# State products on two row halves of the array, gated channel blocks in half-bank pieces, and one FFN block moved between the pairs

## The reference

```python
x_conv = silu(conv1d(x_inner))             # 512 channels
x_dbl  = x_conv @ x_proj_w.T               # 1 + 16 + 16
delta, B, C = softplus(x_dbl[..., 0]), x_dbl[..., 1:17], x_dbl[..., 17:]
h_t = h_{t-1} * exp(delta_t * A) + x_t * (delta_t * B_t)     # 16 states a channel
y_t = h_t @ C_t
y   = (y + x_conv * D) * silu(z)
x   = x + y @ out_proj_w.T
x   = x + ffn(layernorm(x))                # W_exp, butterflies, gelu, butterflies, W_con
```

## Time and profile before

| What | Value |
|---|---|
| median of 3 runs | 578.4 us (578.23 to 579.31) |
| profiled execution, its own time | 576.75 us |
| span of the profiled execution | 575.0 us |
| PE busy | 527.7 us, 92% of the span |
| DVE busy | 407.2 us, 71% |
| ScalarE (ACT) busy | 305.8 us, 53% |
| GpSimd (POOL) busy | 109.4 us, 19% |
| mean granted TensorE clock | 0.961 of full speed |

### The profile page before, as it was taken

The page is one execution under the profiler, slowest core; times in us unless marked ns, Lnnn a source line. Parts: engine busy times, 40 slices in busy tenths (PEclk is TensorE's granted clock), DMA queues, the critical chain, the costliest instruction groups (busy, mean ns, idle before and its releaser), DMA issues.

```text
span 575.0 us, 8152 instructions
## 1 busy us (share of the span) xinstructions
PE 527.7 (92%) x2996; PEld 429.6 (75%) x2996; DVE 407.2 (71%) x860; ACT 305.8 (53%) x526; POOL 109.4 (19%) x96
## 2 busy tenths in 40 slices
PE   4998998398899999999999999999999999789996
PEld 3765766285788878887788779786888788668886
DVE  4852999776994689657983799468957696565532
ACT  3762777577128742686239623873278515551342
POOL 4032100031010411031201311050103111311110
PEclk9985989599999999999999999999999999799999
DMA  8344302010012101120012002110021001200011
GB/s 262 3 26 67 110 12 75 0 40 1 2 38 73 40 2 36 38 77 0 15 61 72 5 2 68 46 38 0 1 74 39 1 2 36 77 1 0 1 38 36
DMA packets 42619, 21.75 MB, mean 38 GB/s; under 512 B 26419, under 2 KB 41011, under 8 KB 42580
## 3 DMA queue, kind: packets, MB, share of 16 engines
q1 hardware_dynamic: 40980, 18.61, 13.7%
q10 hardware_dynamic: 1600, 2.62, 1.2%
HBM read 16.78 MB, written 4.46 MB: 37 GB/s over the span
## 4 chain that ended last, share of the span: by engine, by line
PE 63%; DVE 16%; ACT 10%; issue 6%; DMA 2%; POOL 1%; SPq 1%; DVEq 0%; ACTq 0%; POOLq 0%
PE wide L714 14%; PE acc L847 12%; PE wide L836 10%; PE wide L825 7%; PE wide L814 3%; PE wide L807 2%; DMA b_hat<-in_L_attn_x_proj_w_dram 2%; DVE state L1517 2%; PE small L704 2%; DVE xc L1413 2%; PE wide L724 1%; PE small L734 1%; DVE stats L1308 1%; DVE mixed L1393 1%; PE small L773 1%
## 5 line engine op out<-in xcount | busy, mean ns | idle before, releaser
L1055 ACT ACTIVATE hid_f<-wide,bias_up 128x512 f32<-128x512 f32 x64 | 43.9, 686 | 162.6 <-PE wide L836 162.2
L1413 DVE SCALAR_TENSOR_TENSOR xc<-xi,taps,xc 128x512 f32<-128x512 f32 x96 | 87.0, 911 | 4.2 <-ACT xc L1086 2.0
L847 PE MATMUL acc<-w_down_high,hid_high 128*128 128x256 f32 x256 | 73.2, 286 | 5.8 <-DVE hid_low L1430 5.6
L847 PE MATMUL acc<-w_down_high,hid_low 128*128 128x256 f32 x256 | 72.0, 281 | 0.0
L847 PE MATMUL acc<-w_down_low,hid_high 128*128 128x256 f32 x256 | 72.0, 281 | 0.0
L1430 DVE TENSOR_TENSOR hid_low<-hid_f,hid_high 128x512 fp32r<-128x512 f32 x64 | 46.3, 725 | 28.5 <-ACT hid_high L1164 28.0
L714 PE MATMUL wide<-xnT_ln1T_high,w_in_high 128*128 128x512 f32 x128 | 57.0, 445 | 2.3 <-DVE xnT_ln1T_low L1424 2.3
L836 PE MATMUL wide<-xnT_ln2T_high,w_up_high 128*128 128x512 f32 x128 | 55.4, 433 | 3.4 <-DVE xnT_ln2T_low L1424 1.8
L524 POOL TENSOR_TENSOR rstd<-var_eps,minus_half 128x4 f32<-128x4 f32 x16 | 19.1, 1193 | 200.5 <-DVE var_eps L1318 200.5
L825 PE MATMUL wide<-w_out,xc 128*128 128x256 f32 x256 | 56.7, 379 | 0.1
L847 PEld LDWEIGHTS acc<-w_down_high,hid_high 128*128 128x128 f32 x256 | 48.1, 188 | 11.4 <-issue 8.5
(11 more groups left out here) (185 smaller groups left out, 1058.2 us busy)
## 6 DMA issues: line engine op xcount, KB each, us to landing
x_res<-in_L_attn_x_dram SPq DMA_DIRECT2D x9, 512.0 KB, 3.5
c_near<-c_of_tokens SPq DMA_DIRECT2D x8, 512.0 KB
out_dram<-x1b_xn SPq DMA_DIRECT2D x8, 512.0 KB, 2.9
x_ln<-in_L_attn_x_dram SPq DMA_DIRECT2D x7, 512.0 KB, 3.5
xc<-in_L_attn_in_proj_w_dram ACTq DMA_DIRECT2D x2, 512.0 KB, 6.3
xc<-in_L_ffn_W_exp_dram ACTq DMA_DIRECT2D x1, 1024.0 KB, 9.2
low_w<-in_L_ffn_W_con_dram SPq DMA_DIRECT2D x1, 1024.0 KB, 5.8
raw_out<-n_L_attn_out_proj_w_dram ACTq DMA_DIRECT2D x1, 512.0 KB, 10.1
```

Of the source, the lines that this page charges most:

```text
L847: last = pe.matmul(acc[:, c, :], hid[h][:, j % HRING, c * P:(c + 1) * P], w_down[w][:, j, 0:DM], start=j == 0 and c % 2 == 0 and n == 0, s ...
L1055: ins = act.activation(out_ap, in_ap, how.pop("func"), **how)
L1413: ins = dve.scalar_tensor_tensor(xc[u % BATCH][:, e, :], xi[:, e, tap:tap + TILE], taps[:, e, tap:tap + 1], xc[u % BATCH][:, e, :], ALU.mu ...
```

## The change

A pair of channel blocks now shares two banks by halves of the tokens: bank h of the pair holds tokens 256h to 256h+255 of both blocks. A state product is split into two, h = 0 on rows 0 to 63 of the state and of `c_startT` with the tokens 0 to 255, h = 1 on rows 64 to 127 with the tokens 256 to 511; they write different banks. `ssm_output` is called once for each pair, and in a phase `up` 3 and `down` 1 stand between the two calls (not in `first_phase`). `WIDE_ORDER` follows. `gate` reads a block in two operations of 256 tokens, one from each bank, and a pair's banks come free with the second block's `gate`.

```diff
-    WIDE_ORDER += uses(("up", range(3)), of=phase - 1) + uses(("y", range(CB)), of=phase)
-    WIDE_ORDER += uses(("up", range(3, 5)), of=phase - 1) + uses(("out", range(2)), of=phase)
+    WIDE_ORDER += uses(("up", range(3)), of=phase - 1) + uses(("y", range(2)), of=phase)
+    WIDE_ORDER += uses(("up", [3]), of=phase - 1) + uses(("y", range(2, CB)), of=phase)
+    WIDE_ORDER += uses(("up", [4]), of=phase - 1) + uses(("out", range(2)), of=phase)
...
+            def ssm_output(u, pair):
+
+                banks = [tile_of("y", 2 * pair + h, u) for h in range(2)]
+                for h in range(2):
+                    free(pe, u, "y", 2 * pair + h)
...
+                for q in range(2):
+                    g = 2 * pair + q
+                    for c in range(GR):
+                        at = q * HALF_TILE + c % 2 * P
+                        pe.matmul(banks[c // 2][:, at:at + P], x_tok[:, c, g * P:(g + 1) * P],
+                                  m_mat[:, c * P:(c + 1) * P], start=q == 0 and c % 2 == 0, stop=False,
+                                  skip_group_check=True)
...
+                for q in range(2):
+                    g = 2 * pair + q
+                    for h in range(2):
+                        rows = slice(2 * SLOT * h, 2 * SLOT * (h + 1))
+                        last = pe.matmul(banks[h][:, q * HALF_TILE:(q + 1) * HALF_TILE],
+                                         state[u % BATCH][rows, g * P:(g + 1) * P],
+                                         c_startT[rows, h * HALF_TILE:(h + 1) * HALF_TILE],
+                                         start=False, stop=q == 1, skip_group_check=True)
+                        if q == 1:
+                            mark_written(last, "y", 2 * pair + h, u)
...
                 down(p, 0)
-                ssm_output(u)
+                ssm_output(u, 0)
                 up(p, 3)
                 down(p, 1)
+                ssm_output(u, 1)
                 up(p, 4)
                 down(p, 2)
...
             def gate(u, g):
...
+                for h in range(2):
+                    tokens = slice(h * HALF_TILE, (h + 1) * HALF_TILE)
+                    if q == 0:
+                        written(dve, u, "y", 2 * pair + h)
+                    ins = dve.scalar_tensor_tensor(y[:, tokens], y[:, tokens], skip[:, g:g + 1],
+                                                   tile_of("y", 2 * pair + h, u)[:, q * HALF_TILE:(q + 1) * HALF_TILE],
+                                                   ALU.mult, ALU.add)
+                    if q:
+                        mark_read(ins, "y", 2 * pair + h, u)
+                        read(dve, u, "y", 2 * pair + h)
+                    else:
+                        link(ins)
                 dve.tensor_tensor(y, y, z[u % BATCH][:, g, :], ALU.mult).then_inc(gated.handle, 1)
```

More of the change, by code:

```diff
@@ L53 @@
 SLOT = 32
+HALF_TILE = TILE // 2
 HALF = P // 2
@@ L796, in off_diagonal @@
                 mark_written(last, "moff", 0, u)
[L798 to L815, removed]
+            def ssm_output(u, pair):
+                banks = [tile_of("y", 2 * pair + h, u) for h in range(2)]
+                for h in range(2):
+                    free(pe, u, "y", 2 * pair + h)
+                if pair == 0:
+                    read(pe, u, "moff", 0)
+                for q in range(2):
[5 more added lines that the diff above has]
+                                  skip_group_check=True)
+                if pair == 0:
+                    read(pe, u, "ct", 0)
+                    wait(pe, first_state, u, 1)
+                    wait(pe, states_ready, u, 1)
+                for q in range(2):
[8 more added lines that the diff above has]
+                            mark_written(last, "y", 2 * pair + h, u)
@@ L903, in first_phase @@
                 prepare(13)
-                ssm_output(0)
+                ssm_output(0, 0)
+                ssm_output(0, 1)
                 prepare(14)
@@ L1548, in gate @@
             def gate(u, g):
+                pair, q = divmod(g, 2)
                 y = xc[u % BATCH][:, g, :]
```

## The result

The change is slower: a median of **592.53 us** (589.71 to 593.02, 4 runs) against 578.48 us of the kernel before (578.23 to 579.31, 4 runs), a ratio of 1.0256 with a 95% interval of 1.0215 to 1.0297. That is some 14 us more; the forecast was 587.9 (9.5 more), in a range of 578.0 to 597.0. The execution with the profile took 592.97 us (span 591.3). All ratios leave out two executions that fell in a slower state of the chip: 643.04 us of experiment 1, the one with the profile there, and 585.41 us of run 6.

What follows compares the result with a forecast made beforehand. DVE's list from `gate` 0 on was taken as the bound, with no slack. Phases 1 to 5 +7.9, phase 0 +1.7, phase 6 +0.6 and phase 7 -0.7 gave +9.5 us: 587.9, range 578.0 to 597.0.

Steps and rivals of the forecast that it cites:

- DVE's list has no slack from `gate` 0 to `low_hidden` 6: Phases 1 to 5: added DVE length makes the phase end late; PE's earlier saving is waited away at `down` 6.
- d = 1.00 us a pair: Time of a pair's state products on row halves, between 0.86 and 1.72; PE saves 0.72 us a pair.
- A PE wait of 2 us or more at `down` 6: Sign that the forecast is right: late in a phase, PE waits this long for `low_hidden` 6.
- Phases 1 to 5, +7.9: Each of these phases ends 1.58 us late: 1.10 at `gate` 2 and 0.48 from `gate` 2 and 3.
- The likeliest case: DVE bounds the kernel and row halves run side by side: chance 0.60, forecast 587.9 us.
- Phase 0, +1.7: No FFN block between the pairs; the second pair waits for `gate` 1's first half; 1.7 us added.
- Phase 6, +0.6: `low_hidden` 6 ends 1.1 us after PE wants it, of which 0.5 is lost in waits for ACT.
- Phase 7, -0.7: From `gate` 0 to the output projection 9.1 us against 9.8; kept, with nothing behind it on DVE.
- PE was the bound: Rival: DVE's delay has slack behind it, 16 pairs save 0.72 us each, 566.9 us; chance 0.12.
- A lower granted clock: Rival: longer waits ahead of the second pair and at `down` 6 slow TensorE; not in the sum; chance 0.07.
- Halves in turn: Rival: row halves do not run side by side, a pair takes 1.72 us; +17.1, 595.5 us; chance 0.13.
- The lateness is small: Rival: `gate` halves at 0.37 and pairs at 0.86 leave 0.6 a phase, about +2.4, 580.8 us; no separate chance.

Runs made afterwards that it cites:

- experiment 1: The change with `ssm_output(u, 1)` directly behind `ssm_output(u, 0)`, ahead of `up` 3 and `down` 1, as in the old order: 605.07 us.
- run 6: Kernel before with crossed row halves, `up` 3 and `down` 1 between the pairs, and DVE's `low_hidden` 6 and 7 ahead of `second_normalise`: 581.96 us.
- Experiment 4: Kernel before with each `gate`'s first operation split into two of 256 tokens, nothing else: 584.03 us.
- Experiment 5: Kernel before with row halves alone, crossed between a pair's two blocks, a semaphore between the turns; banks and gates as before: 578.84 us.
- experiment 3: The change with each state product on all 128 rows; same banks and split gates: 591.05 us.
- experiment 8: The change with DVE's `low_hidden` 6 and 7 ahead of `second_normalise`: 588.44 us.
- experiment 9: The change with the setup product `prepare(14)` between the two calls of `first_phase`: 590.58 us.
- experiment 11: The change with DVE's `first_residual` and `low_hidden` 6 and 7 moved ahead of `low_parts` and `second_normalise`: 581.87 us.
- experiment 12: The change with DVE's list rearranged further, two transposes behind the output projection, and `prepare(14)` between phase 0's pairs: 578.20 us.
- run 10: Kernel before with `up` 3 and `down` 1 between the pairs, and DVE's `first_residual`, `low_hidden` 6 and 7 ahead of `low_parts` and `second_normalise`: 573.81 us.

## Why the prediction was right, and where its sum was short

- **DVE's list has no slack from `gate` 0 to `low_hidden` 6: right.** Experiment 4 added four times 0.24 us a phase to DVE alone, and the phase grew by 0.97. Experiment 5 took some 0.3 us of PE time away alone, and got nothing.
- **`gate` in halves, 0.48 each, 0.24 more a `gate`: right.** The halves take 1.00 us for two, and the next `gate` comes 1.65 us after (220.75 to 222.40); the forecast was 1.63.
- **d = 1.00 us a pair: too low, with the products around it counted.** The passes themselves take 1.06 us to the next product (218.45 to 219.51). But 1.72 on full rows less the 0.46 that experiment 3 shows is 1.26. Beyond the 0.86 of a full overlap that leaves 0.40, which I put down to the change to row halves and back; from the column quarters I had read 0.13. The 1.12 us that the prediction had as an estimate by the Trainium skill ("TensorE: Matmul & The Clock Gate", Measured speedup) was nearer than my reading, and still too low. The size hardly mattered, since `gate` 2 starts before the pair is complete.
- **The second pair waits for `gate` 1, and `gate` 2 for the pair: right.** The pair started 2.78 us after `gate` 0 (forecast 2.67), `gate` 2 waited 0.65 (forecast 0.62). PE's own wait there was shorter than the 1.2 forecast, 0.89 in the profile, since it came later out of the first pair and the FFN block.
- **A PE wait of 2 us or more at `down` 6: right in sum, wrong in place.** PE waited 1.53 at `up` 6 and 0.46 at `down` 6, together 1.99. I had followed `low_hidden` 6 alone and not the ring's bank that `first_residual` 0 gives to `up` 6. Both lie on DVE's list behind `gate` 3, so the lateness was the same; experiments 6 and 8 show what it costs to know only one of the two.
- **Phases 1 to 5, +7.9: measured +8.5.** The likeliest case was the right one.
- **Phase 0, +1.7: measured +5.7, the step that failed.** The wait for `gate` 1 was right: the second pair started 2.26 us after `gate` 0 (forecast 2.16). But the sum priced the pair at full clock. It ran at the low one, the rival that "the sum has nothing for", and took 2.74 us more; `gate` 2 came 8.05 us after `gate` 0 (81.31 to 89.36), where I had 5.26. Six traces have the change's banks (the change, experiments 3, 8, 9, 11 and 12), and in all six this pair ran slow (token products 2.68 to 3.75 us); in the seven with whole banks it did not (1.95 to 2.32, in one lot or two). So the low clock goes with the change's banks; that PE's wait causes it isn't shown, since in experiment 9 the wait was 0.58 us and the pair slow all the same. The 5.7 is on the high side: from `gate` 0 to `gate` 0 phase 0 took 74.46 to 76.13 us in those six, 70.54 to 72.01 in the six with whole banks and whole gates.
- **Phase 6, +0.6: measured +2.4.** Up to the second norm the steps came as worked out: `low_hidden` 6 ended at 26.1 us after `gate` 0 (499.3 less 473.22), forecast 26.2. The other 1.4 us lie after it, in phase 7's front part, where the low clock lasted longer and cost 1.66 us. That stretch was slow in six of 13 traces, with and without the change's banks, so it is not the change's doing; without it the phase came out as forecast.
- **Phase 7, -0.7: measured -0.2.**

By parts, then: 4.0 us of the shortfall in phase 0, 0.6 in phases 1 to 5, 1.8 in phase 6, 0.5 in phase 7, together 6.8 of the traces' 16.3 (rounded parts). Of these, the 1.66 us of phase 7's front part are not the change's. By medians it is 4.6 us (592.53 less 587.9), because the profiled execution of before lay 1.7 us below its median, and that of after 0.4 above.

The rivals: "PE was the bound" (566.9) falls with experiment 4, and experiment 5 agrees. "A lower granted clock" did come in, in phase 0. "Halves in turn" falls with experiment 3's rows, and its price of 595.5 was too high: on full rows the kernel takes 591.05. "The lateness is small" falls with the gates' 0.48.

## What to carry to other kernels

A busy share of 92% and the largest part of the chain did not make PE the bound where the change was made: its waits were short and ended on one engine's list, which had no slack between the points where the two meet. Before pricing a change on the engine that looks full, add a piece to the other engine alone, and list every place where the first waits for the second, banks in a ring included. A new order of that list, read off those waits, gave 0.67% with whole rows and the FFN block between the pairs (run 10), where halving the products gave nothing that the runs can tell (experiment 5).

## What the runs showed of the hardware beyond what I expected

- A pair's eight passes on row halves saved 0.46 us of PE, 0.40 less than half of their 1.72 (experiment 3 against the change); column quarters had shown a loss of 0.13.
- Crossed into shared banks, with a semaphore between the turns, the same eight passes took 1.43 us to the next product (experiment 5), not 1.06 (218.45 to 219.51 in the change).
- A PE idle time of 3.38 us in phase 0 was followed by a granted clock of 0.50 and a pair 2.74 us longer; the idle times of 0.89 and 1.53 us in phases 1 to 5 left the clock at 1.00. Idle time is not the whole of it: the kernel before shows 0.57 from 76 to 80 us with PE busy throughout.
- The same wait cost differently from one trace to the next. Behind PE's idle time of 3.68 us in phase 7's front part the clock read 0.50 in all 13 traces (without experiment 1), for 5 to 6 us in seven of them and for 10 to 11 us in six.
